# A fourth bank and reordered norms in the joining phase, and joined pieces, other reloads and another VectorE order in the last phase of a two-layer network

## The reference

```
q = conv4(x @ Wq); k = conv4(x @ Wk); v = conv4(x @ Wv)      # third: causal depthwise, 4 taps
q, k, v = silu(q), silu(k) * D ** -0.5, silu(v)
alpha, beta = sigmoid(x @ Wa + ba), sigmoid(x @ Wb + bb)
...
logits = x.reshape(b, -1) @ switch_w.T + switch_b            # fourth: one choice for a sequence
gate, top_idx = top_k(softmax(logits), 2)
h = gelu(x_heads @ w1[top_idx] + b1[top_idx])                # 16 heads of 32 features, 2 experts
o = (h @ w2[top_idx] + b2[top_idx]) * gate                   # summed over the 2 experts
out = (x + o) @ w3.T + b3
x = x + layernorm(out)
```

## Time and profile before

| what | us |
|---|---|
| median of 3 runs | 2785.55 |
| the runs | 2784.3 to 2785.78 |
| profiled execution, its own time | 2788.34 |
| its span in the trace | 2786.6 |

### The profile page before, as it was taken

The page is one execution under the profiler, slowest core; times in us unless marked ns, Lnnn a source line. Parts: engine busy times, 40 slices in busy tenths (PEclk is TensorE's granted clock), DMA queues, the critical chain, the costliest instruction groups (busy, mean ns, idle before and its releaser), DMA issues. The chain is left out here.

```text
span 2786.6 us, 37729 instructions
## 1 busy us (share of the span) xinstructions
PE 2710.6 (97%) x13269; PEld 1515.8 (54%) x13270; DVE 1754.9 (63%) x4341; ACT 1216.8 (44%) x2256; POOL 604.5 (22%) x662
## 2 busy tenths in 40 slices
PE   8999999999999989999999999999999999999998
PEld 3444444445655455666566665666566665664432
DVE  5767763011111477777787778777787778735986
ACT  4645441111121355455654556445554556333243
POOL 1112101401111412033313332133312332020000
PEclk9999999999999989999999999999999999999999
DMA  4101025013214741002110021101210011127313
GB/s 137 51 1 46 28 94 209 31 68 123 68 64 155 293 183 35 16 32 77 66 43 31 32 73 65 46 17 46 69 69 31 32 43 65 61 93 270 110 50 106
DMA packets 76555, 217.92 MB, mean 78 GB/s; under 512 B 11968, under 2 KB 12896, under 8 KB 67296
## 3 DMA queue, kind: packets, MB, share of 16 engines
q1 hardware_dynamic: 58224, 171.61, 17.2%
q0 software_dynamic: 8944, 27.30, 3.1%
q10 hardware_dynamic: 9216, 16.78, 1.6%
HBM read 162.02 MB, written 53.65 MB: 77 GB/s over the span
## 5 line engine op out<-in xcount | busy, mean ns | idle before, releaser
L2572 DVE SCALAR_TENSOR_TENSOR c_conv<-c_ps_pj,c_conv_t,c_conv 128x511 f32<-128x511 f32 (+2 forms) x450 | 335.7, 746 | 33.4 <-ACT c_conv L2391 22.8
L2065 POOL TENSOR_SCALAR c_gate<-c_gate 128x512 f32<-128x512 f32 x64 | 37.8, 618 | 983.3 <-DVE c_block_L L2605 983.3
L2141 PE MATMUL c_ps_pj<-c_xs,c_w_v 128*128 128x512 f32 x480 | 225.9, 593 | 0.0
L2141 PE MATMUL c_ps_pj<-c_xs,c_w_q 128*128 128x512 f32 x360 | 173.0, 610 | 0.0
L2162 PE MATMUL c_ps_pj<-c_w_g,c_xs 128*128 128x512 f32 x384 | 172.7, 592 | 0.0
L2141 PE MATMUL c_ps_pj<-c_xs,c_w_k 128*128 128x512 f32 x360 | 165.2, 595 | 0.0
L2391 ACT ACTIVATE c_conv<-c_ps_pj,c_conv_t 128x512 f32<-128x512 f32 x150 | 116.3, 776 | 50.1 <-issue 28.6
L2454 ACT ACTIVATE c_err<-c_negL 32x128 f32<-32x128 f32 x256 | 78.6, 307 | 134.5 <-DVE c_negL L2638 129.8
L1373 DVE TENSOR_TENSOR x_act<-x_hs,x_ps_u 128x352 f32<-128x352 f32 x36 | 18.7, 521 | 173.4 <-ACT x_hs L1358 173.4
L2602 DVE TENSOR_TENSOR c_block_X<-c_block_X,c_block_t 128x58 f32<-128x58 f32 (+6 forms) x448 | 117.6, 262 | 15.4
L2599 DVE TENSOR_TENSOR c_block_t<-c_block_L,c_block_X 128x58 f32<-128x58 f32 (+6 forms) x448 | 117.4, 262 | 14.9
(11 more groups left out here) (617 smaller groups left out, 5995.2 us busy)
## 6 DMA issues: line engine op xcount, KB each, us to landing
c_G<-cum_d SPq DMA_DIRECT2D x16, 1024.0 KB, 4.7
c_xs<-xt_d SPq DMA_DIRECT2D x16, 1024.0 KB, 4.8
ot_d<-c_oT ACTq DMA_DIRECT2D x64, 256.0 KB, 2.0
b_w_gu<-in_w_gu SPq DMA_DIRECT2D x8, 1408.0 KB, 21.1
y_slots<-x_y SPq DMA_DIRECT2D x36, 256.0 KB, 2.0
d_x<-x SPq DMA_DIRECT2D x32, 256.0 KB, 3.0
d_switch<-in_switch_w SPq DMA_DIRECT2D x4, 2048.0 KB
a_x<-in_x SPq DMA_DIRECT2D x7, 1024.0 KB, 7.3
```

The source lines that it names most:

```text
L2141: mm = e.matmul(bank_of[xb][u][:, :], w["kqv"[u // HG]][:, k, (u % HG) * DH:(u % HG + 1) * DH], xs[xb][:, k, :], start=(k == 0), stop=(k = ...
L2572: e.scalar_tensor_tensor(oc, bank_of[buf][u][:, 0:SEQ - s], conv_t[buf][:, m, h, TAPS - 1 - s:TAPS - s], oc, ALU.mult, ALU.add).then_inc(c ...
```

## The change

In the joining phase, one of the two `cum` banks becomes a fourth bank for the units (`unit_ps`), ahead of the three; the end's four matmuls now wait until the unit in that bank is through, and stand before the last unit. A unit's start waits for the tap of the unit four before, and units 0 and 1 wait only for the `down` pieces that used their bank. On TensorE units 2, 4, 5 and 8 move ahead of what they followed (transposes, gate logits). On ScalarE tap 2 stands before `take_turned(1)`, and taps 4 and 5 before the copy of the first running sum. On VectorE the z addition of block 0 moves ahead of `residual(2)`, taps 3 ahead of `sums(3)`, taps 5 ahead of `x_shift(3)`.

In the last phase, blocks 2 and 3 do half the features at a time: `four_hidden(b, q)` is 8 matmuls of 32 partitions by 64 columns into four banks (the two `h` banks, the transposes' bank and the logits' bank), `four_outputs(b, q)` 8 matmuls of 64 partitions by 32 columns. Their weights are the plain selected ones (`w1_four`, `w2_four`), so the 4 small instructions for the pairs go in `choose(2)` and `choose(3)`. The last layer cycles two banks, not three. Blocks 1 to 3 of x are loaded again into the table `switch`, which is free by then, all 12 tiles at once. The last tile's scaling goes from ScalarE to VectorE (`finish_end`), the statistics of a block get a second tile (`z_mvs`), and VectorE's order is another.

```diff
+        unit_ps = [cum_pairs[1][:, :, :].rearrange("p k m -> p (k m)")] + [pj[i][:, :] for i in range(PJ)]
...
-                if u >= PJ:
-                    e.wait_ge(conv_step, T1 * (u - PJ + 1))
-                elif u == 0:
-                    e.wait_ge(down_copied, len(downs))
+                if u >= len(unit_ps):
+                    e.wait_ge(conv_step, T1 * (u - len(unit_ps) + 1))
+                elif u > 0:
+                    e.wait_ge(down_copied, len(downs) - 2 + min(u, 2))
...
             e.wait_ge(row0_copied, 1)
             e.wait_ge(logs_done, NG)
+            e.wait_ge(conv_step, T1 * 9)
...
+            unit(11)
             e.wait_ge(cum_copied, 1)
...
-            residual(2)
-            x_shift(2)
             e.wait_ge(ab_loaded, 32)
             e.wait_ge(z_ready, 1)
...
-            taps(1)
-            taps(2)
+            residual(2)
+            x_shift(2)
+            for u in range(1, 4):
+                taps(u)
             e.wait_ge(soft0_step, 3)
...
             sums(3)
             y_shift(3)
-            taps(3)
...
             taps(4)
             residual(3)
+            taps(5)
             x_shift(3)
...
+        four = [h_ps[0][:, :], h_ps[1][:, :], turned_bank, l_bank[:, :]]
+        head_rows = [slice(i * FH, (i + 1) * FH) for i in range(HB)]
+        pairs_of = 2 * KD * FOURS
+        z_ps = [yo[m % 2][:, :] for m in range(NT)]
...
+        again = lambda b, c: x[c][:, :] if b == 0 else switch[:, b, c * DM:(c + 1) * DM]
...
             for c in range(TPB):
-                load_again(c)
+                load_again(0, c)
+            e.wait_ge(switched, NE * NT)
+            for b in range(1, NB):
+                for c in range(TPB):
+                    load_again(b, c)
             for n in range(NT):
                 store_out(n)
-                if n + TPB < NT:
-                    load_again(n + TPB)
...
+            def four_hidden(b, q):
+                p = KD // 2 * (b - FOURS) + q
+                if p == 0:
+                    e.wait_ge(xt_done, NT)
+                if q == 0:
+                    e.wait_ge(route, ROUTE_STEPS * (b + 1))
+                e.wait_ge(gelu_done, pairs_of + HB * p)
+                for i, rows_ in enumerate(head_rows):
+                    for j, of_dc in enumerate(half_rows):
+                        mm = e.matmul(four[i][of_dc, :], w1_four[b][rows_].rearrange("p k f -> p (k f)"), XT[rows_, b, 2 * q + j, :],
+                                      start=True, stop=True)
+                    mm.then_inc(h_ready, 1)
+
+            def four_outputs(b, q):
+                p = KD // 2 * (b - FOURS) + q
+                e.wait_ge(mixed_done, KD * b + 2 * q)
+                e.wait_ge(gelu_done, pairs_of + HB * (p + 1))
+                for i, rows_ in enumerate(head_rows):
+                    for j, of_dc in enumerate(half_rows):
+                        mm = e.matmul(o_ps[j][rows_, :], w2_four[b][of_dc, :], given.conv[of_dc, i, :], start=True, stop=True)
+                        if i == HB - 1:
+                            mm.then_inc(o_ready, 1)
...
+            for b in range(1, NB - 1):
                 last_layer(b, 0)
-                hidden_layer(b + 1, 0)
+                four_hidden(b + 1, 0)
                 last_layer(b, 1)
...
+                four_outputs(b + 1, 0)
+                four_hidden(b + 1, 1)
                 last_layer(b, 2)
...
+                four_outputs(b + 1, 1)
+                last_layer(b, 3)
...
+            def finish_end():
+                c = TPB - 1
+                zc, z_mv = z[(NB - 1) % 2][c][:, :], z_mvs[(NB - 1) % 2]
+                e.tensor_scalar(zc, zc, z_mv[:, c, 0:1], None, ALU.subtract).then_inc(z_offset, 1)
+                e.wait_ge(z_offset, TPB)
+                e.wait_ge(z_rstd, TPB)
+                e.scalar_tensor_tensor(again(NB - 1, c), zc, z_rs[:, c:c + 1], again(NB - 1, c), ALU.mult, ALU.add).then_inc(out_done, 1)
```

More of the change, by code:

```diff
@@ L1594, in _ @@
             unit(1)
+            unit(2)
             turn(1)
-            unit(2)
             gate_logits(0)
@@ L1688, in _ @@
             tap(1)
+            tap(2)
             take_turned(1)
-            tap(2)
             scale_y(2)
@@ L1722, in _ @@
                 e.activation(flat(tab[name]), cum_ps[i + 1], ACT.Exp).then_inc(tables_done, 1)
+            tap(11)
             e.wait_ge(rows_ready, 1)
@@ L1808, in _ @@
             residual(3)
+            taps(5)
             x_shift(3)
-            for u in range(5, 9):
+            for u in range(6, 9):
                 taps(u)
@@ L3018, in gelus, with four_gelus @@
                         e.activation(hidden[:, dc % 2, i, :], h_ps[i][:, :], ACT.Gelu, bias=b1_sel[:, b:b + 1]).then_inc(gelu_done, 1)
+            def four_gelus(b, q):
+                p = KD // 2 * (b - FOURS) + q
+                e.wait_ge(o_ready, KD * b + 2 * q)
+                for i in range(HB):
+                    e.wait_ge(h_ready, pairs_of + HB * p + i + 1)
+                    e.activation(given.conv[:, i, :], four[i], ACT.Gelu, bias=b1_sel[:, b:b + 1]).then_inc(gelu_done, 1)
             def scale_z(b):
@@ L3055, in _ @@
             e.preload_act_table_set("gelu_and_others")
-            for b in range(2, NB):
-                gelus(b, range(2))
-                scale_z(b - 2)
-                gelus(b, range(2, KD))
+            for b in range(FOURS, NB):
+                four_gelus(b, 0)
+                four_gelus(b, 1)
+                scale_z(b - FOURS)
             scale_z(NB - 2)
@@ L3130, in route_back, with choose @@
                 assert m + 2 == ROUTE_STEPS * b + ROUTE_BACK
-            def choose(b):
+            def choose(b, part=range(2)):
                 m = ROUTE_STEPS * b + ROUTE_BACK
@@ L3259, in _ @@
             mix(1, [2, 3])
-            last_root(0)
             route_back(3)
             last_norm(1, 0)
-            choose(3)
+            last_root(0)
             last_norm(1, 1)
-            mix(2, [0])
+            mix(2, [0, 1])
+            choose(3, [0])
+            mix(2, [2, 3])
             last_norm(1, 2)
-            mix(2, [1])
+            choose(3, [1])
+            last_norm(1, 3)
             finish(0)
-            mix(2, [2])
-            last_norm(1, 3)
-            mix(2, [3])
+            last_norm(2, 0)
             last_root(1)
-            last_norm(2, 0)
             last_norm(2, 1)
-            mix(3, [0])
+            mix(3, [0, 1])
             last_norm(2, 2)
-            mix(3, [1])
+            mix(3, [2, 3])
             finish(1)
-            mix(3, [2])
             last_norm(2, 3)
-            mix(3, [3])
             last_root(2)
-            finish(2)
-            for c in range(TPB):
-                last_norm(NB - 1, c)
-                if c > 0:
-                    shift_last(c - 1)
-                if c > 1:
-                    finish(NB - 1, [c - 2])
-            shift_last(TPB - 1)
-            finish(NB - 1, [TPB - 2, TPB - 1])
+            last_norm(3, 0)
+            finish(2, [0, 1])
+            last_norm(3, 1)
+            shift_last(0)
+            finish(2, [2, 3])
+            last_norm(3, 2)
+            shift_last(1)
+            finish(3, [0])
+            last_norm(3, 3)
+            shift_last(2)
+            finish(3, [1, 2])
+            finish_end()
 def program(nc, io):
```

143 lines of the change are left out of this document (76 added, 67 removed).

## The result

| | median us | runs | ratio to before, 95% interval |
|---|---|---|---|
| before | 2784.93 | 6, from 2782.66 to 2788.97 | |
| changed | 2771.03 | 6, from 2769.46 to 2772.63 | 0.9948, 0.9937 to 0.9958 |

The change saves 13.9 us. 2766.5 was forecast, with a range of 2759 to 2774. The profiled execution of the changed kernel took 2769.46 us (span 2767.7), the shortest of its six; that of before took 2788.34, 3.4 above this median. So the two traced executions lie 18.9 us apart where the medians lie 13.9.

The account below looks back on a forecast made before the run. TensorE's list bounds the last phase; in the joining phase nothing is full. 14.0 us (last phase) plus 5.0 (joining) off 2788.3 gives 2769.3, or 2766.5 against the median 2785.55; own range 2763 to 2771, wide range 2759 to 2774.

Parts of the forecast that it names:

- rival (1): The joining phase gives nothing: the logarithms' wait, longer idle time and slow clock eat it; 2771.5 us, chance 0.13.
- A group of eight: Last phase, blocks 2 and 3, TensorE: eight tiles side by side take 1.15 us a group; 7.4 us saved.
- The others can follow: Last phase: VectorE, nearly full, and ScalarE keep up with TensorE; no wait, 0.8 us to spare at the tightest.
- The end: Last phase, from TensorE's end to the span's: 7.4 us instead of 12.3, with x already there; 4.9 saved.
- steps (a) to (e): Joining phase's x chain, from unit 0's earlier start to x_shift(3), forecast to end at 1027.2, 1.8 us ahead.
- (c): Joining phase: block 0's logarithms sit behind take_turned(2); VectorE gets them at 1003.0, sums(3) starts 0.8 us later.
- Step (f): Joining phase's end: 3.4 us less work behind the last transposes; next phase at 1054.6 instead of 1059.79, 5 us gained.
- 5.0: The joining phase's whole forecast gain in us; bounds 1.5 with two more slow stretches, 9 at best.
- (d): Joining phase: y_shift(3) at 1014.0, residual(3) 3.5 us ahead, its adds meeting GpSimd's; adds before those would gain 3 more.

Follow-up runs that it names:

- e8: Changed kernel with x's reloads chained to the stores again, as before the change; groups and VectorE's order kept: 2786.14 us (one run).
- e5: Changed kernel with unit 9 ahead of the last block's gate logits on TensorE: 2768.19 us.
- e4: Changed kernel with GpSimd's additions to G waiting until residual(3) has added all four tiles: 2765.73 us.
- e1: Kernel before with the change's joining phase alone: 2787.29 us.
- e7: Changed kernel with blocks 2 and 3 of the last phase in 16 pairs again, VectorE's mixes and ScalarE's gelus placed for them: 2780.98 us.
- e3: Changed kernel with eight more 512-column matmuls, whose results nothing reads, between unit 8 and the last block's transposes: 2770.69 us.

## Why the prediction was right, and where it was not

The measured 2771.03 lies in the stated range because that range was drawn over rival (1), which is what happened; the forecast's own range, 2763 to 2771, just misses it. The last phase came out by the mechanism that was forecast, with one step wrong, and the joining phase did not.

- **A group of eight** was taken at 1.15 us; it takes 1.03. The mechanism held (the eight tiles ran side by side and cost no more than two), and the price stood nearer to the lower bound. By the figure for nine tiles in the Trainium skill ("TensorE: Matmul & The Clock Gate", Part 3) it would, as an estimate, have been 1.4; its tiles are 32 by 32, and for these shapes the measurement decides. Eight groups: 8.3 us where 9.2 was forecast. TensorE's list gave 10.1, not 9.1.
- **The others can follow**: right. TensorE never waited, though VectorE was busy for 22.2 to 22.8 of 25 us.
- **The end** was forecast at 7.4 us (its terms add up to 7.3) and is 7.0. But the step behind it was wrong, and the total hides that: 9.1 for TensorE and 4.9 for the end were added as two gains of their own. e8 shows that the reload chain was a second bound of the phase, not an item of 4.9 us: with the chain kept, the groups and the new order gave 1.6 us. The rows of before that would have told it are SyncE's of this phase, which the prediction doesn't use:

```profile
2753.33 0.34 SPq L2809 DMA_DIRECT2D out<-d_x  x1
...
2780.64 0.32 SPq L2805 DMA_DIRECT2D d_x<-x  x1
```

  There the chain runs from 2753.33 to the end in steps of 3.6 us.
- **Joining, steps (a) to (e)** held within 1.6 us: on the time scale of before (adding the 2.3 us by which the trace lies earlier), the logarithms came at 1002.6 (forecast 1003.0), the adds at 1015.4 (1016.4), x_shift(3) at 1025.6 (1027.2), and the last block was turned and copied at 1032.8 (1032.7). TensorE waited 8.1 us, not 6.6. The wait in (c) is there (VectorE stood 2.78 us for the logarithms) and cost nothing, since y_shift(3) came when ScalarE's root behind tap 7 let it.
- **Step (f) failed**, and it is the missing gain. "Gate logits 1036.3, two units and 1.0 slow 1044.2" gave 11.5 us from the transposes to the units' end; it was 16.1 (1030.48 to 1046.6), 4.6 more. The prediction had seen that TensorE "pays in clock", but priced it at 1.0 and left the gate logits at full speed (3.6), where they took 7.01 and the two units 2.3 more than at full clock. In the old order a unit stood there, during which the clock came back; the change had moved it away. e5 gives it back.
- **The base.** 5.0 was also taken from a trace whose joining stretch was 3.2 us longer than a second trace of the same code. The prediction took the 2.8 us by which the profile exceeded the median off the total, but counted the stretch's gain from rows that held this excess.
- **The number** was 4.5 us too low: the last phase gave 1.4 more than forecast in the traces, the joining phase nothing. Rival (1), 2771.5, is what happened, by two of the three things that it named, the longer idle time and the slow clock. The 1.5 us between the last phase's 15.4 in the traces and the 13.9 of the medians are within what runs differ by.
- The contention with GpSimd in (d) was priced at 3 us; e4 shows 3.0 in the adds' row, 3.7 in the stretch, and 5.3 in the median.

## What to carry to other kernels

Ask of every stretch not only how long an engine is idle but what stands behind the idle time: here 512-column units ahead of 32-column matmuls took 4.7 us less than the other way round. When two chains end within a few microseconds of each other (here TensorE's list and the store-and-reload chain), shortening one is worth little until the other is shortened too (1.6 and 5.1 us alone, 15.4 together); read the DMA-issuing queue's rows like an engine's. And before counting a gain from a stretch of one profile, ask whether the excess of that profile over the median lies in that very stretch.

## What the hardware showed that was not expected

- 16 float32 matmuls of 32 columns, back to back, ran at 1.2 GHz for all of their 7.0 us without the granted clock rising (changed kernel, e1, e4, e7, e8), and in e3 the clock fell during them, though the profile shows TensorE as busy throughout.
- Eight tiles side by side, with 512 columns in float32, took 1.02 to 1.05 us with the switch to the next piece, no more than two tiles (1.01 and 1.06).
- A store, the wait for it, a load and the next store in one SyncE queue take 3.64 us for a tile of 128 by 512 values (e8; 3.60 before).
- A VectorE instruction of 128 by 4 values with both inputs in SBUF took 0.81 us when it began inside a GpSimd addition and 0.15 where it fell between two (e4), while one with an input in PSUM (the taps) kept its 2.3 us for three.
